# A macaron block on one core: the last batch's merge moved behind the thirteenth block of the last group, and the last two blocks added to the output's table in turn

## The reference, cut to what matters

```python
B, S, D, H, E = (4, 512, 512, 256, 8)          # the feed-forward part; two experts of eight for each token
    logits = xf @ gate_w
    top_logits, top_idx = jax.lax.top_k(logits, K)          # K = 2
    top_gates = jax.nn.softmax(top_logits, axis=-1)
    gates = jnp.sum(jax.nn.one_hot(top_idx, E, dtype=xf.dtype) * top_gates[..., None], axis=1)
    h = gelu(jnp.einsum('nd,edh->neh', xf, w1) + b1)
    out_e = jnp.einsum('neh,ehd->ned', h, w2) + b2
    routed = jnp.einsum('ne,ned->nd', gates, out_e)
    shared = gelu(xf @ shared_w1 + shared_b1) @ shared_w2 + shared_b2
    return (routed + shared).reshape(B, S, D)
...
x = x + 0.5 * _L0_ffn_ref(_layernorm(x, axis=-1), ...)
x = x + _L0_attn_ref(_layernorm(x, axis=-1), ...)
x = x + 0.5 * _L0_ffn_ref(_layernorm(x, axis=-1), ...)   # the change is at the end of this one
```

## Time and profile before

| | us |
|---|---|
| median of 3 runs | 1135.01 |
| lowest and highest | 1130.98, 1138.28 |
| the profiled execution | 1135.68 |
| its span, first to last instruction | 1134.4 |

### The profile page before, as it was taken

The page is one execution under the profiler, slowest core; times in us unless marked ns, Lnnn a source line. Parts: engine busy times, 40 slices in busy tenths (PEclk is TensorE's granted clock), DMA queues, the critical chain, the costliest instruction groups (busy, mean ns, idle before and its releaser), DMA issues. The chain is left out here.

```text
span 1134.4 us, 11728 instructions
## 1 busy us (share of the span) xinstructions
PE 1033.2 (91%) x3552; PEld 573.8 (51%) x3552; DVE 733.9 (65%) x1232; ACT 641.0 (57%) x1125; POOL 513.2 (45%) x463
## 2 busy tenths in 40 slices
PE   5988999978899999999989989999989959999994
PEld 2466545554355554455554443466556435564672
DVE  2230015886899979999989988999987971202000
ACT  4344324669557585568687464468589535262442
POOL 3446521362653442654362128445473733345443
PEclk9989999899999999999999988999999979999998
DMA  9956754695666577765786772367887564555566
GB/s 317 327 159 147 117 121 141 131 250 120 134 183 158 166 159 147 189 178 121 180 208 113 198 205 57 112 184 172 164 199 181 108 169 100 84 101 102 130 98 88
DMA packets 71058, 176.24 MB, mean 155 GB/s; under 512 B 13090, under 2 KB 13090, under 8 KB 68870
## 3 DMA queue, kind: packets, MB, share of 16 engines
q0 software_dynamic: 34144, 76.11, 37.5%
q1 hardware_dynamic: 35558, 89.76, 26.0%
q10 hardware_dynamic: 1296, 9.63, 2.4%
HBM read 114.71 MB, written 70.17 MB: 163 GB/s over the span
## 5 line engine op out<-in xcount | busy, mean ns | idle before, releaser
L1717 POOL DMA_INDIRECT xs<-x_normal,rows_i x113 | 128.5, 1137 | 235.4 <-PE xps L904 181.8
L913 PE MATMUL hps<-w_all,hidden_sb 128*128 x904 | 224.2, 393 | 11.5 <-ACT hidden_sb L1095 8.5
L929 PE MATMUL yps<-w_all,hidden_sb 128*128 x452 | 215.3, 601 | 6.3 <-ACT ys L1108 4.1
L913 PEld LDWEIGHTS hps<-w_all,hidden_sb 128*128 128x128 f32 x904 | 170.8, 197 | 52.6 <-issue 32.6
L1517 DVE TENSOR_TENSOR_SCAN run<-pwx,trig 128x512 f32<-128x512 f32 x128 | 149.5, 1209 | 33.4 <-ACT trig L1183 33.2
L1741 POOL DMA_INDIRECT x_rows<-ys,rows_i x60 | 105.4, 1757 | 118.2 <-ACT ys L1108 105.1
L871 PE MATMUL yps<-sw_sb,hidden_sb 128*128 128x512 f32 x256 | 121.0, 616 | 0.0
L1108 ACT ACTIVATE ys<-yps,slots 128x512 f32<-128x512 f32 x113 | 78.0, 691 | 75.1 <-PE yps L929 44.1
L929 PEld LDWEIGHTS yps<-w_all,hidden_sb 128*128 128x128 f32 x452 | 81.0, 192 | 73.9 <-issue 71.8
L859 PE MATMUL hps<-xnT,sw_sb 128*128 128x512 f32 x256 | 117.0, 609 | 0.0
L1078 ACT COPY hidden_sb<-xps 128x512 f32<-128x512 f32 x113 | 65.8, 584 | 64.9 <-PE hps L913 43.0
(11 more groups left out here) (201 smaller groups left out, 1532.3 us busy)
## 6 DMA issues: line engine op xcount, KB each, us to landing
qx<-q_cols SPq DMA_DIRECT2D x64, 512.0 KB
w_all<-in_w_experts SPq DMA_DIRECT2D x8, 1024.0 KB
x_normal<-xin SPq DMA_DIRECT2D x32, 256.0 KB, 2.1
xin<-x_rows SPq DMA_DIRECT2D x32, 256.0 KB
turns_sb<-in_w_out ACTq DMA_DIRECT2D x3, 1536.0 KB
xin<-in_x SPq DMA_DIRECT2D x16, 256.0 KB
sum_rows<-ys SPq DMA_DIRECT2D x16, 256.0 KB
xin<-sum_rows POOLq DMA_DIRECT2D x16, 256.0 KB, 6.0
```

The source lines that it names most:

```text
L913: t = PE.matmul(hps[:, bank, 0:H], xT[:, j % 2, c, :], w_all[:, bass.ds(expert[j] + c * H, H)], start=c == 0, stop=c == KC - 1)
L929: t = PE.matmul(yps[:, bank, :], hb[:, j % 2, ec, :], w_all[:, bass.ds(expert[j] + (KC * H + ec * D), D)], start=ec == 0, stop=ec == EC - 1)
L1717: GE.indirect_dma_start(xs[:, j % NX, :], None, xn_rows[PAIR_OF[g]], bass.IndirectOffsetOnAxis(rows_i[:, g % 2, j:j + 1], 0)).then_inc(*xs ...
```

## The change

For group 6 alone, the batch's merge is waited for after blocks 11 and 12, the last on either side so far, and stands behind block 12's add. Block 13's add waits for the merge and goes to the output. Block 14's add waits for block 13's and goes to the output as well, with `into_i`; before, it went to `x1_rows`. The other edits give the planner the same dependencies and costs.

```diff
                 if j >= 2:
                     last = [("POOL", ("add", g, j - 2), 4.3)]
+                    if g == NG - 1 and j == NB - 2:
+                        last += [("POOL", ("m_out", JOBS[z][1]), -2.6)]
...
-                piece("POOL", ("add", g, j), 1.65, ("ACT", s), *last)
+                ends = g == NG - 1 and j == NB - 1
+                piece("POOL", ("add", g, j), 6.65 if ends else 1.65, ("ACT", s), *last)
             if JOBS[z][0] == 2:
+                merged = NB - 2 if g == NG - 1 else NB
                 for q in GROUPS[g]:
-                    piece("POOL", ("m_out", JOBS[q][1]), 1.0, ("POOL", ("add", g, NB - 1), 3.8),
-                          ("POOL", ("add", g, NB - 2), 3.8))
+                    piece("POOL", ("m_out", JOBS[q][1]), 1.0, ("POOL", ("add", g, merged - 1), 3.8),
+                          ("POOL", ("add", g, merged - 2), 3.8))
...
                 pool.wait_ge(*ys_kept.at((g, j)))
-                if j >= 2:
+                if g == NG - 1 and j >= NBS[g] - 2:
+                    b = JOBS[LAST[g]][1]
+                    pool.wait_ge(*out_merged[b].at(b))
+                    if j == NBS[g] - 1:
+                        pool.wait_ge(*y_added[1 - side].at((g, j - 1)))
+                elif j >= 2:
                     pool.wait_ge(*y_added[side].at((g, j - 2)))
...
-                at = into_i if side else rows_i
-                GE.indirect_dma_start(INTO[g][side], bass.IndirectOffsetOnAxis(at[:, g % 2, j:j + 1], 0),
+                table = 1 if g == NG - 1 and j >= NBS[g] - 2 else side
+                at = into_i if table else rows_i
+                GE.indirect_dma_start(INTO[g][table], bass.IndirectOffsetOnAxis(at[:, g % 2, j:j + 1], 0),
                                       ys[:, j % 2, :], None, compute_op=ALU.add).then_inc(*y_added[side].of((g, j)))
...
             def merge_output(b):
-                for end in blocks_added(GROUP_OF[B + b]):
-                    pool.wait_ge(*end)
+                g = GROUP_OF[B + b]
+                if g == NG - 1:
+                    for j in (NBS[g] - 4, NBS[g] - 3):
+                        pool.wait_ge(*y_added[j % 2].at((g, j)))
+                else:
+                    for end in blocks_added(g):
+                        pool.wait_ge(*end)
```

## The result

The changed kernel takes 1137.85 us in the median of 20 runs (1130.88 to 1146.25), the kernel before 1133.55 in the median of 20 (1129.35 to 1141.32). The ratio is 1.0042, with a 95% interval of 1.0022 to 1.0063. So it is slower by 0.42%, which is 4.8 us with an interval of 2.5 to 7.1, and well within 1%; the two medians lie 4.3 us apart. The forecast was +3.06 us (0.27%) and a time of 1138.1.

What follows compares the result with a forecast made beforehand. TensorE, 91% busy, bounds the kernel, but only the tail moves: -7.16 us of cover plus two adds of 4.72 + 0.39 gives +3.06, on the median of 1135.01 about 1138.1 us; range 1134.0 to 1143.0.

Steps and rivals of the forecast that it cites:

- Only the end moves: Whole program: instruction order is unchanged on every engine but for POOL's last three, so only the tail can move.
- The cover gained, 7.16 us: Tail: the merge is released by block 12's buffer at 1113.74 instead of block 14's at 1120.90, 7.16 us earlier.
- The merge for itself, 8.12 us: Merge in its new place: has the DMA engines for itself, so takes its undisturbed 8.12 us.
- Rival 2: Early merge: lands slower beside ACT and TensorE, up to 10.3 us, adding 2.2, giving 1140.2 us; chance 0.13.
- The landing time of an add, 4.72 us: Adds of blocks 12, 13 and 14: each lands 4.72 us after issue; the change breaks even at 3.19.
- Rival 1: Last adds: short enough, under 3.19 us each, that the early merge pays; chance 0.07.
- rival 3: Two adds behind the merge: slow, 7.82 us instead of 4.72, giving +9.26 and 1144.3 us; chance 0.04.
- The handoff, 0.39 us: POOL's tail: 0.39 us from each landing to the next issue, before the merge and both later adds.
- the 23.72 us of the prediction: Forecast tail, from block 12 in its buffer at 1113.74 to the last add landed at 1137.46.
- What is queued behind the merge: POOL's queue: only the adds of blocks 13 and 14 stand behind the merge, awaited only by SP at the end.
- The signs given: Changed profile: POOL idle about 7.5 and 3.6 us before the last two adds, span near 1137.5.
- the 3.6 named as the point of change: Last two add issues: under 3.6 us apart would mean the change gains and the prediction is wrong.

Runs made afterwards that it cites:

- the second execution: The changed kernel, unaltered, profiled once more to see how well its tail repeats: 25.42 us from the end of ACT's write of block 12 to the end.

## Why the prediction was right, point by point

- **Only the end moves.** Right. The order is the same up to POOL's last three, and the timed loss, 4.8 us (2.5 to 7.1), agrees with that of the tail, 4.2 to 4.9.
- **The time, 1138.1 against 1137.85.** That it came this close is luck. The forecast started from 1135.01, the median of three runs, and the median of 20 is 1133.55, 1.5 us lower. The loss was forecast at 3.06 us, and the medians lie 4.3 apart, 1.2 more. The two errors cancel.
- **The cover gained, 7.16 us.** Right: in the changed kernel block 12's write ends at 1109.05 and block 14's at 1116.18, 7.13 us apart.
- **The merge for itself, 8.12 us.** Right: 7.91 and 8.14 in the two executions. Rival 2, a slower merge in the new place, fell.
- **The landing time of an add, 4.72 us.** Near: 4.78 for block 12's and 4.75 for block 13's; 5.06 for block 13's in the second execution. I called the row of 4.72 one of an idle chip, and it wasn't, since block 13's add overlapped it; but in the changed kernel the adds that ran alone took no less, 4.75 and 5.06. Rival 1 needed under 3.19, rival 3 needed 7.8; both fell. By the Trainium skill's fit (DMA: Bandwidth & Descriptors, Anatomy of one DMA), with its estimate of 2.6 us, the change would have gained 1.2; the measured adds decide against that estimate.
- **The handoff, 0.39 us: the mis-sized term.** I took one row, that of the merge before, for all three. There the waits stand in the cheaper order, and the step ahead of a direct merge is shorter than that ahead of an indirect add (0.54 to 0.65 against 0.75 to 0.88 with the waits in the same order). Measured were 0.54, 0.88 and 0.75 us, 1.0 us more in sum. With 0.25 more for the last add (4.97 to the end, of which 4.8 to its landing), 0.21 less for the merge and 0.09 more for the two other adds the 23.72 us of the prediction become 24.85. With the waits turned the tail came to 23.60 and 23.27, close to the 23.72, with handoffs ahead of the adds on both sides of 0.39 and a shorter last add.
- **What is queued behind the merge.** Right: nobody waits for it but the two adds.
- **The signs given.** Idle times of 7.80 and 3.90 us before the two adds, against 7.5 and 3.6 forecast. The last two issues are 5.50 us apart, over the 3.6 named as the point of change. The other sign of being wrong was a merge that takes over 9 us between its issue and the next: it was 8.79 in the first execution and 9.02 in the second. The merge isn't the cause, since it landed after 8.14 us there; the 0.88 us of handoff is, and I had not left room for it in that sign. The span, 1133.9 instead of 1137.5, was a poor sign to give, since what lies ahead of the tail scatters by more than the whole effect.

## What to carry to other kernels

Moving a long transfer off the end pays only if what must then run behind it, one after the other, is shorter than the cover that is gained. Here two dependent adds of 128 rows, 4.8 us and a handoff each, stood against 3.6 us of matrix products per block; with the two last adds side by side in two tables, the tail behind the same early merge was 3.3 us shorter, and still 0.9 longer than with the merge at the end. And where the effect is a fraction of what whole executions scatter by, measure the tail from an event that both kernels share.

## What the runs showed that I had not expected

The order in which an engine waits for several semaphores has a price when a transfer is what ends last. With a wait already fulfilled standing last, 0.27 us pass from an add's landing to POOL's next add and 0.4 to 0.5 from the merge's landing to the next add (waits turned, each twice), and 0.39 ahead of the merge (before, twice). With the wait for the transfer itself standing last, it is 0.75 to 0.88 us ahead of an add and 0.54 to 0.65 ahead of the merge. Turning the waits made it shorter ahead of the adds of the changed kernel and longer in the one before. Ahead of a merge the number of pieces seems to count as well, with 0.29, 0.39 and 0.58 us for 128, 256 and 512; but there is only one execution for the first and the last. What POOL's sequencer does in that time these runs don't show, nor why the last add, too, was 0.3 us shorter with the waits turned.
